# Cross-attention and a routed FFN on one core: x plus bias ahead of time, two chunk buffers, sums of P in turns

## The chip, the cores and the metric

One Trainium2 chip, one of its cores. The metric is the device time of the kernel in microseconds (us). The engines are TensorE (PE in rows; PEld are its weight loads), VectorE (DVE), ScalarE (ACT), GpSimd (POOL, here Pool) and SyncE (SP), which here only issues DMAs.

## What is computed

```python
x = x + xattn(ctx, layernorm(x))     # latents = layernorm(x): 2048 x 256; context 1601 x 192, masked
x = x + ffn(layernorm(x))            # 8 experts, the best 2 of each token

# xattn: 4 heads of 64
q = ln @ Wq.T;  k, v = split(concat([xn @ Wkv.T, ln @ Wlkv.T]))
attn = softmax(mask(rmsnorm(q, qn_g) * SCALE @ rmsnorm(k, kn_g).T))
out = (attn @ v) @ Wo.T + bo
# ffn
w, idx = top_k(softmax(x @ router.T), 2);  w = w / (w.sum() + 1e-6)
y = sum over the 2 experts of w * ((silu(x @ w1) * (x @ w3)) @ w2)
```

All arrays are float32.

## The kernel before

The kernel is written engine by engine, each with its own program in a fixed order; semaphores tie them together. NT = 16 tiles of 128 tokens, NC = 13 tiles of context, NK = 29 tiles of keys (context, then the latents themselves), NP = 15 pairs of key tiles.

*Prologue* (to about 160 us). For each of the 29 key tiles, in a pipeline of steps: normalise, transpose, project, write K^T (tiles S1, S2), V, and for latents Q^T (QT). x is loaded in one DMA into V[:, NC:NK], and ScalarE overwrites each of those tiles with its V (L532). Pool writes the mask column of each context tile (`k_mask`, L396 to 404) and waits for the transpose before the last in each step.

*Attention* (to about 840 us): UNITS = 16 units, u = 4 b + h: block b of 512 queries (QB = 4 tiles), head h. In each unit a loop over the 15 pairs p:

- TensorE: scores of pair p into one of two PSUM tiles bS (two products per key tile, L1238 and L1239), then, in odd steps, the products of P with V of pairs p-3 and p-2 (`outputs`, L1249). Between them stand 32 "pieces" of the score maxima of the *next* unit (`piece`, L1169), into two banks bM; VectorE reduces each (L862), and piece k waits for the reduction of piece k-2.
- ScalarE: P = exp(scores) into one of NPT = 4 buffers PT (L644). Before it may write buffer p % 4 it waits for the product with V of pair p-4 and for the sum that read it (`pt_free`, L597).
- The sum of P over keys, for the softmax: Pool adds pairs 0 to 10 into acc_p (ten instructions, L417, as `POOL_SUMS` says), VectorE adds pairs 11 to 14 into acc_d after its work on pieces (three instructions, L894), then merges the two (L900, L902).
- Weight splitting, six chunks of 128 x 256 per unit: SP loads a chunk of the expert weights into wraw[n % 2] (L323); ScalarE rounds it into whi (`w_hi`, L611, after the exponential of the pairs in `SPLIT_AT`), SP stores whi; Pool writes the rest, wraw - whi, into wraw (`w_lo`, L419, after the sums in `LO_AT`), SP stores that and then loads chunk n+2. `w_hi(n)` waits for chunk n's load, for the store of whi of chunk n-1 and for `w_lo(n-1)`.
- At p = 5 the output of the unit before is transposed and normalised (`o_T`, `o_out`); at p = 7 in even units two heads are transposed (`heads_T`, L1191) and ScalarE copies them into QT (L595), after its `w_hi` of that step.
- In units of blocks 1 to 3 (`w.fin`) one tile t of the block before is finished: x is loaded (`x_load`, p = 1, on ScalarE's queue), Pool adds the bias (L432), TensorE projects at p = 8 (L1196), VectorE adds and takes statistics (`stats2`, L907 to L911), ScalarE takes the square root (`sd`, p = 9, after its `w_hi`; the table of functions is loaded for it and again for the next exp), VectorE normalises at p = 10 (L917), TensorE transposes x3 at p = 11 (L1202), ScalarE copies it as x3T (L658, after its `w_hi`), TensorE multiplies by the router at p = 12 (L1208).

*Tail* (to about 912 us). The last QB = 4 tiles take the same steps together: SP loads x after the last product with V (L342 to L344), Pool adds the bias and makes the iotas (L439 to L450), and VectorE waits for the iotas first and then takes `stats2` and `norm` for each. ScalarE meanwhile issues the loads of the split weights of experts 0 to 3 (12.6 MB) ahead of its copy of the last output (L669 to L675). Then a long chain on VectorE routes the tokens (L972 to L1065), with the large table G at L1031.

*FFN* (to the end): 39 blocks of 128 rows: gather, three products per projection, scatter with add.

## Time and profile before

| | us |
|---|---|
| median of 3 runs | 1138.31 (1138.18 to 1139.41) |
| the profiled execution, its own time | 1141.2 |
| its span | 1139.2 |
| TensorE busy in the span | 983.2 (86%) |
| Pool, VectorE, ScalarE busy | 594.1, 653.5, 477.6 |

The rows further down are read like this. Times count from the span's start. An instruction in order of time has its start, its length, engine, line, operation and the tiles it writes and reads; `x8` means that eight were merged; in brackets stands how long the engine had been idle before it and who released it. "DMA x<-y" as a releaser is a transfer. A matmul's end is modelled, so the matmuls of a row overlap the next. 128x1024 is partitions by elements.

### The profile page before, as it was taken

Reading aid. Unit: us, or ns where it says so; the run is one execution under the profiler, and the core shown is the slowest. Engines: PE = TensorE matmul, PEld = TensorE weight load, DVE = VectorE, ACT = ScalarE, POOL = GpSimd, SP = SyncE. Lnnn points to the kernel's source line nnn. Section 1 sums busy time; section 2 is a strip of 40 time slices with the busy share of each in tenths; the row PEclk is TensorE's granted clock in tenths of the full one; section 3 lists DMA queues with packets and bytes.
Section 4 is the critical chain, followed back from the end, with each engine's and each line's share of the span. In section 5 each row is a group of like instructions: output and inputs, shape, how many; then the busy total and the mean of one; then the engine's idle time right before and its main releaser. Section 6 shows DMA issues by size and latency. Waiting matters only on the chain.

```text
span 1139.2 us, 15241 instructions
## 1 busy us (share of the span) xinstructions
PE 983.2 (86%) x4556; PEld 638.2 (56%) x4557; DVE 653.5 (57%) x1311; ACT 477.6 (42%) x751; POOL 594.1 (52%) x460
## 2 busy tenths in 40 slices
PE   2799779999999899898999999999882469999994
PEld 2565445555555555555554554555442458888883
DVE  3889776666666566566566566566125624444442
ACT  1456524455445446445455545454431022233231
POOL 4000018766974864854955855846820025556552
PEclk9899879999999999999999999999975579999998
DMA  6000002112111212121112212122169093332332
GB/s 173 1 1 1 9 5 72 54 56 70 61 61 65 71 55 70 57 69 65 61 61 70 65 56 75 56 65 75 56 262 367 16 360 48 54 51 51 51 52 27
DMA packets 66240, 85.15 MB, mean 75 GB/s; under 512 B 10283, under 2 KB 62444, under 8 KB 64140
## 3 DMA queue, kind: packets, MB, share of 16 engines
q1 hardware_dynamic: 49166, 56.57, 14.6%
q0 software_dynamic: 7488, 10.23, 5.5%
...
q8 instruction: 27, 0.44, 0.2%
q14 instruction: 25, 0.20, 0.1%
...
## 4 chain that ended last, share of the span: by engine, by line
PE 47%; POOL 20%; issue 10%; ACT 8%; DVE 8%; DMA 5%; ACTq 2%; DVEq 0%; POOLq 0%; SPq 0%
POOL acc_p L417 16%; PE bPV L1249 10%; ACT PT L644 5%; PE bS L1238 4%; PE bM L1169 4%; POOL wraw L421 4%; PE bS L1239 3%; PE bA L1116 3%; DMA x2t<-x 2%; PE bG L1328 2%; DVE mpart L862 2%; PE bH L1345 2%; PE bV L1133 2%; PE bG L1330 1%; PE bG L1329 1%
## 5 line engine op out<-in xcount | busy, mean ns | idle before, releaser
L862 DVE TENSOR_REDUCE mpart<-bM 128x1 f32<-128x464 f32 x492 | 295.6, 635 | 178.8 <-PE bM L1169 177.6
L417 POOL TENSOR_TENSOR acc_p<-acc_p,PT 128x1024 f32<-128x1024 f32 x144 | 343.8, 2387 | 33.6 <-ACT PT L644 29.3
L644 ACT ACTIVATE PT<-bS 128x1024 f32<-128x1024 f32 (+1 forms) x240 | 232.2, 993 | 64.8 <-PE bS L1239 58.4
L1249 PE MATMUL bPV<-PT,V 128*64 128x512 f32 x928 | 233.1, 610 | 0.0
L1238 PE MATMUL bS<-Q,S 128*128 128x512 f32 x464 | 190.0, 409 | 3.8 <-ACT PT L644 1.5
L1169 PE MATMUL bM<-S,Q 128*128 128x464 f32 x492 | 175.1, 414 | 12.1 <-DVE mpart L862 7.0
L1239 PE MATMUL bS<-Q,S 128*128 128x512 f32 x464 | 183.9, 396 | 0.0
L417 POOL TENSOR_TENSOR acc_p<-PT 128x1024 f32<-128x1024 f32 x16 | 41.6, 2601 | 255.9 <-ACT PT L644 255.9
L615 ACT CAST whi<-wraw 128x256 fp32r<-128x256 f32 x96 | 38.9, 405 | 248.3 <-POOL wraw L421 245.1
L1169 PEld LDWEIGHTS bM<-S,Q 128*128 128x128 f32 x492 | 85.0, 191 | 97.4 <-DVE mpart L862 67.6
L1238 PEld LDWEIGHTS bS<-Q,S 128*128 128x128 f32 x464 | 88.2, 190 | 56.6 <-issue 22.7
L1249 PEld LDWEIGHTS bPV<-PT,V 128*64 128x64 f32 x928 | 59.0, 136 | 104.9 <-issue 87.2
L1239 PEld LDWEIGHTS bS<-Q,S 128*128 128x128 f32 x464 | 88.1, 190 | 14.3
L478 POOL DMA_INDIRECT out<-ysb,ring_s x39 | 62.4, 1599 | 41.0 <-POOL ring_s L472 31.3
L421 POOL TENSOR_TENSOR wraw<-wraw,whi 128x256 fp32r<-128x256 f32 x96 | 70.5, 734 | 9.5 <-ACT whi L615 9.5
L1078 DVE TENSOR_TENSOR hs<-hs,bU 128x512 f32<-128x512 f32 x39 | 26.8, 688 | 63.6 <-PE bU L1330 62.1
L460 POOL COPY ring_g<-gidx 128x1 int32 (+1 forms) x39 | 27.6, 708 | 57.2 <-DVE sidx L1065 48.8
L463 POOL DMA_INDIRECT xg<-xln_d,ring_g x39 | 39.5, 1012 | 31.0 <-POOL ring_g L460 30.2
L696 ACT CAST hTe<-bH 128x512 fp32r<-128x512 f32 x39 | 22.9, 587 | 66.9 <-PE bH L1345 57.4
L708 ACT CAST xTe<-bXe 128x256 fp32r<-128x256 f32 x39 | 14.6, 374 | 85.7 <-PE bXe L1366 85.7
L1328 PE MATMUL bY<-W,hTe 128*128 x156 | 47.2, 303 | 1.5 <-DVE hTe L1072 1.5
L1329 PE MATMUL bY<-W,hTe 128*128 x156 | 44.0, 282 | 0.0
...
## 6 DMA issues: line engine op xcount, KB each, us to landing
wraw<-w SPq DMA_DIRECT2D x96, 128.0 KB, 2.3
wsp_d<-whi SPq DMA_DIRECT2D x96, 128.0 KB, 2.2
wsp_d<-wraw SPq DMA_DIRECT2D x96, 128.0 KB, 1.7
...
x<-x ACTq DMA_DIRECT2D x12, 128.0 KB, 2.0
out<-x ACTq DMA_DIRECT2D x12, 128.0 KB, 1.9
```

Of the source, the lines that this page charges most:

```text
L417: pool.tensor_tensor(acc_p[:], one, PT[:, q % NPT, :, :], ALU.add).then_inc(sem("z_p"), 1)
L421: pool.tensor_tensor(wraw[:, n % 2, :].bitcast(F32R), wraw[:, n % 2, :], whi[:].bitcast(F32), ALU.subtract).then_inc(sem("wsplit"), 1)
L463: pool.indirect_dma_start(xg[:, s.par, :], None, xln_d, bass.IndirectOffsetOnAxis(ap=ring_g[:, s.par:s.par + 1], axis=0))\
L478: pool.indirect_dma_start(out, bass.IndirectOffsetOnAxis(ap=ring_s[:, s.par:s.par + 1], axis=0), ysb[:, s.par, :], None, compute_op=ALU.add)\
L644: act.activation(PT[:, p % NPT, 0:n, :], bS[(w.h + p) % 2][:, 0:n, :], ACT.Exp).then_inc(sem("exp"), 1)
L862: dve.tensor_reduce(mpart[:, i, g:g + 1], banks[k % len(banks)][:, 0:PIECE], AX, ALU.max)\
L1169: pe.matmul(banks[k % len(banks)][:, 0:PIECE], Q2[:, h % 2, i * P:(i + 1) * P], S2[:, h, g * PIECE:(g + 1) * PIECE], start=True, stop=True ...
L1238: pe.matmul(bS[sl][:, b, :], S1[:, h, c * P:(c + 1) * P], Q1[:, h % 2, :], start=True, stop=False)
L1239: last = pe.matmul(bS[sl][:, b, :], S2[:, h, c * P:(c + 1) * P], Q2[:, h % 2, :], start=False, stop=True)
L1249: last = pe.matmul(bPV[b * D:(b + 1) * D, 0, :], V[:, c, h * D:(h + 1) * D], PT[:, p % NPT, b, :], start=c < 2, stop=c >= NK - 2, skip_gro ...
L1328: pe.matmul(out_ap, st_hi, w[:, e, 0, lo:lo + n], start=first, stop=False)
L1329: pe.matmul(out_ap, st_lo, w[:, e, 0, lo:lo + n], start=False, stop=False)
```

## The change

- *x plus bias*. In the prologue Pool adds bo to each of the 16 tiles of x, as they stand in V before V overwrites them, into a buffer xbs of two tiles, and SP stores them to a new DRAM tensor xb_d. ScalarE's copy of V for a latent tile waits for the add of that tile. All later loads of x read xb_d, and Pool's adds of the bias in the units and in the tail are gone. The mask loop on Pool is written out instead of looped.
- *Two chunk buffers*. whi has two halves; `w_hi(n)` waits for the store of whi of chunk n-2 and for `w_lo(n-2)`.
- *Early last x tiles*. x2t lies over the Q buffers of even heads, and ScalarE issues its four loads at p = 2 of the last unit. VectorE waits for the stores out of x2t before it writes G.
- *Sums*. Pool takes pairs (0, 1), 2, 3, 6, 7, 8, 10, 11, 12 (nine instructions), VectorE (4, 5), 9, 13, 14 (four), the first two of them at p = 7 and p = 11 of its loop, ahead of the reductions of that step. `w_lo` goes after Pool's sums number 1, 2, 3, 5, 6, 8 (counted from 0) instead of 1, 3, 5, 7, 9, 9.

```diff
@@ -108,6 +108,7 @@
           router_t, w13, w2, out):
+    xb_d = nc.dram_tensor("xb_d", [TOK, DIM], F32, kind="Internal").ap()
     xln_d = nc.dram_tensor("xln_d", [TOK, DIM], F32, kind="Internal").ap()
@@ -179,7 +180,6 @@
         rt = sb("rt", [P, 2, E], at=big)
-        bob = sb("bob", [P, DIM], at=big)
         lg = sb("lg", [P, NT, E], at=big)
@@ -189,6 +189,8 @@
         qn = sb("qn", [P, 2, DIM], at=t0)
+        bob = sb("bob", [P, DIM], at=t0)
+        xbs = sb("xbs", [P, 2, DIM], at=t0)
         m_u8 = sb("m_u8", [P, NC], U8, at=t0)
@@ -204,17 +206,19 @@
         t1 = ExitStack()
-        Q1 = sb("Q1", [P, 2, QW], F32R, at=t1)
-        Q2 = sb("Q2", [P, 2, QW], F32R, at=t1)
+        tq = ExitStack()
+        QQ = sb("QQ", [P, 2, 2, QW], F32R, at=tq)
+        Q1, Q2 = QQ[:, :, 0, :], QQ[:, :, 1, :]
+        tq.close()
+        x2t = sb("x2t", [P, 2 * QB, DIM], at=t1)
         PT = sb("PT", [P, NPT, 2, QW], at=t1)
...
         wraw = sb("wraw", [P, 2, WC], at=t1)
-        whi = sb("whi", [P, WC], F32R, at=t1)
+        whi = sb("whi", [P, 2, WC], F32R, at=t1)
         t1.close()
...
         t2 = ExitStack()
-        x2t = sb("x2t", [P, QB, DIM], at=t2)
         x3t = sb("x3t", [P, QB, DIM], at=t2)
@@ -308,6 +312,12 @@
+            xb = xb_d.rearrange("(t p) d -> t p d", p=P)
+            for t in range(NT):
+                sp.wait_ge(sem("xb"), t + 1)
+                sp.dma_start(xb[t, :, :], xbs[:, t % 2, :]).then_inc(sem(f"xb_st{t % 2}"), 16)
             sp.wait_ge(sem("klo"), NK)
@@ -327,7 +337,7 @@
                 sp.wait_ge(sem("whi"), n + 1)
-                sp.dma_start(wsp_d[e, 0, :, c:c + WC], whi[:].bitcast(F32)).then_inc(sem("wst_h"), 16)
+                sp.dma_start(wsp_d[e, 0, :, c:c + WC], whi[:, n % 2, :].bitcast(F32)).then_inc(sem(f"wst_h{n % 2}"), 16)
                 sp.wait_ge(sem("wsplit"), n + 1)
@@ -335,13 +345,9 @@
-            xt = x.rearrange("(t p) d -> t p d", p=P)
             ot = out[0:TOK, :].rearrange("(t p) d -> t p d", p=P)
...
             NF = NT - QB
-            sp.wait_ge(sem("pv"), NP * UNITS)
-            for i in range(QB):
-                sp.dma_start(x2t[:, i, :], xt[NF + i, :, :]).then_inc(sem(f"xin_t{i}"), 16)
             for i in range(QB):
@@ -397,11 +403,23 @@
                 pool.wait_ge(sem("mcol"), 1)
-                held()
                 pool.tensor_copy(knat[:, t.par, :, D + 1], mcol[:, bass.ds(t.v, 1)].to_broadcast([P, H]))\
...
-            run_steps(pool, 0, NC + 2, k_mask)
+            def x_bias(t):
+                if t >= 2:
+                    pool.wait_ge(sem(f"xb_st{t % 2}"), 16 * (t // 2))
+                pool.tensor_tensor(xbs[:, t % 2, :], V[:, NC + t, :], bob[:], ALU.add).then_inc(sem("xb"), 1)
+            pool.wait_ge(sem("c_bo"), 16)
+            for t in range(NC + 2):
+                k_mask(Step(None, t))
+                if t == 3:
+                    pool.wait_ge(sem("x_in"), 16)
+                if t >= 3:
+                    x_bias(t - 3)
+            for t in range(NC - 1, NT):
+                x_bias(t)
@@ -418,7 +436,7 @@
                 pool.wait_ge(sem("whi"), n + 1)
-                pool.tensor_tensor(wraw[:, n % 2, :].bitcast(F32R), wraw[:, n % 2, :], whi[:].bitcast(F32),
+                pool.tensor_tensor(wraw[:, n % 2, :].bitcast(F32R), wraw[:, n % 2, :], whi[:, n % 2, :].bitcast(F32),
                                    ALU.subtract).then_inc(sem("wsplit"), 1)
@@ -427,18 +445,11 @@
                             w_lo(SHARE * w.u + k)
-                    if n == XB_AT and w.fin:
-                        pool.wait_ge(sem("xin"), 16 * w.tile + 16)
-                        pool.tensor_tensor(x2[:], x2[:], bob[:], ALU.add).then_inc(sem("xb"), 1)
-            pool.wait_ge(sem("c_bo"), 16)
             run_units(unit)
...
             pool.wait_ge(sem("pv"), NP * UNITS)
-            NF = NT - QB
-            for i in range(QB):
-                pool.wait_ge(sem(f"xin_t{i}"), 16)
-                pool.tensor_tensor(x2t[:, i, :], x2t[:, i, :], bob[:], ALU.add).then_inc(sem("xb"), 1)
             pool.iota(iot_i[:], pattern=[[1, P]], base=0, channel_multiplier=0).then_inc(sem("iota"), 1)
@@ -529,6 +540,8 @@
                     act.wait_ge(sem("v_mm"), t.v + 1)
+                    if b == 'l':
+                        act.wait_ge(sem("xb"), t.back(NC).v + 1)
                     act.copy(V[:, bass.ds(t.v, 1), :].rearrange("p a d -> p (a d)"), bV[t.par][:, 0, 0:DIM])\
@@ -610,13 +623,19 @@
                 act.wait_ge(sem(f"raw{n % 2}"), 16 * (n // 2) + 16)
-                after(act, sem("wst_h"), 16 * n)
-                after(act, sem("wsplit"), n)
-                act.copy(whi[:], wraw[:, n % 2, :]).then_inc(sem("whi"), 1)
-            xt = x.rearrange("(t p) d -> t p d", p=P)
+                after(act, sem(f"wst_h{n % 2}"), 16 * (n // 2))
+                if n > 1:
+                    act.wait_ge(sem("wsplit"), n - 1)
+                act.copy(whi[:, n % 2, :], wraw[:, n % 2, :]).then_inc(sem("whi"), 1)
+            xt = xb_d.rearrange("(t p) d -> t p d", p=P)
             ot = out[0:TOK, :].rearrange("(t p) d -> t p d", p=P)
             xlt = xln_d.rearrange("(t p) d -> t p d", p=P)
+            def x_load_last():
+                act.wait_ge(sem("s_mm"), NP * (UNITS - 1))
+                for i in range(QB):
+                    act.dma_start(x2t[:, i, :], xt[NT - QB + i, :, :]).then_inc(sem(f"xin_t{i}"), 16)
@@ -646,6 +665,8 @@
                         x_load(w.tile)
+                    if p == 2 and w.last:
+                        x_load_last()
                     if p in SPLIT_AT:
@@ -660,14 +681,16 @@
+            for k in range(2):
+                act.wait_ge(sem(f"xb_st{k}"), 16 * NT // 2)
             q_hi(0, 0, 0)
...
-            act.wait_ge(sem("wst_h"), 16 * E * NCH)
             for k in range(2):
+                act.wait_ge(sem(f"wst_h{k}"), 16 * E * NCH // 2)
                 act.wait_ge(sem(f"wst{k}"), 16 * E * NCH // 2)
@@ -902,7 +925,6 @@
             def stats2(t, x_, y, st, mv):
-                dve.wait_ge(sem("xb"), t + 1)
                 dve.wait_ge(sem("y_mm"), t + 1)
@@ -922,7 +944,10 @@
                         o_out(u, (w.h - 1) % H, w.pairs)
+                    if p in DVE_AT:
+                        z_sum(w, DVE_AT.index(p))
                     if p == Y_AT and w.fin:
+                        dve.wait_ge(sem("xin"), 16 * t + 16)
                         stats2(t, x2[:], bT[:, 0, 0:DIM], st2[:], mv2[:])
@@ -939,7 +964,7 @@
                     maxima(v)
-                for n in range(ND):
+                for n in range(DVE_AT.index(NP), ND):
                     z_sum(w, n)
@@ -961,6 +986,7 @@
                 if i < QB:
+                    dve.wait_ge(sem(f"xin_t{i}"), 16)
                     stats2(NF + i, x2t[:, i, :], bFY[i][:, 0, 0:DIM], st2t[:, i, :], mv2t[:, i, :])
@@ -1028,6 +1054,7 @@
             R = 2 * NT
+            dve.wait_ge(sem("ox_t"), 16 * QB)
             link(dve.tensor_tensor(G[:], flat.unsqueeze(2).to_broadcast([P, R, NBLK + 1]),
@@ -1396,10 +1423,10 @@
 OUT_AT, HEADS_AT, Y_AT, SD_AT, X3_AT, X3T_AT, LG_AT = 5, 7, 8, 9, 10, 11, 12
-XB_AT = 2
-SPLIT_AT, LO_AT = (1, 3, 5, 7, 9, 11), (1, 3, 5, 7, 9, 9)
-POOL_SUMS = ((0, 1),) + tuple((-1, p) for p in range(2, 11))
-DVE_SUMS = ((11, 12), (-1, 13), (-1, 14))
+SPLIT_AT, LO_AT = (1, 3, 5, 7, 9, 11), (1, 2, 3, 5, 6, 8)
+POOL_SUMS = ((0, 1),) + tuple((-1, p) for p in (2, 3, 6, 7, 8, 10, 11, 12))
+DVE_SUMS = ((4, 5), (-1, 9), (-1, 13), (-1, 14))
+DVE_AT = (7, 11, NP, NP)
 assert sum(sum(x) for x in PIECES) == NM and len(PIECES) == NP
```

## Rows read from the trace of the kernel before

**Rows 1.** Busy time by stretch: stretch, length, busy us (instructions) per engine, TensorE clock, DMA.
```profile
237.70:276.40 38.70, 38.59 (x175) 22.35 (x174) 25.51 (x42) 19.13 (x27) 28.25 (x16) 1.00 0.20 63
...
489.70:533.50 43.80, 40.93 (x185) 23.71 (x186) 26.96 (x48) 22.60 (x31) 28.76 (x17) 1.00 0.19 63
```

**Rows 2.** TensorE in order of time, an even unit: start, length, instruction [idle before, releaser].
```profile
507.06 0.39 PE L1238 MATMUL bS<-Q,S 128*128 128x512 f32 x1
...
514.99 1.10 PE L1196 MATMUL bT<-wot,QT 128*128 128x256 f32 x4 [1.44 <-ACT QT L595]
...
516.14 0.40 PE L1238 MATMUL bS<-Q,S 128*128 128x512 f32 x1
...
517.88 0.48 PE L1169 MATMUL bM<-S,Q 128*128 128x464 f32 x1 [0.44 <-DVE mpart L862]
...
527.84 0.61 PE L1208 MATMUL bT<-rt,x3T 128*128 128x8 f32 x4 [0.86 <-ACT x3T L658]
```

**Rows 3.** TensorE in order of time, an odd unit.
```profile
478.46 0.44 PE L1202 MATMUL bT<-ident,x 128*128 128x128 f32 x2 [1.32 <-DVE x L917]
...
484.05 0.61 PE L1208 MATMUL bT<-rt,x3T 128*128 128x8 f32 x4 [1.15 <-ACT x3T L658]
```

**Rows 4.** ScalarE in order of time, the even unit of rows 2.
```profile
513.96 0.40 ACT L615 CAST whi<-wraw 128x256 fp32r<-128x256 f32 x1 [3.27 <-POOL wraw L421]
...
517.27 1.02 ACT L644 ACTIVATE PT<-bS 128x1024 f32<-128x1024 f32 x1 [1.50 <-PE bS L1239]
...
527.11 0.40 ACT L615 CAST whi<-wraw 128x256 fp32r<-128x256 f32 x1 [2.41 <-POOL wraw L421]
```

**Rows 5.** SP's DMA issues in that unit; then the page's row: count, KB, us to landing.
```profile
502.32 0.32 SPq L332 DMA_DIRECT2D wsp_d<-wraw  x1
504.39 0.33 SPq L323 DMA_DIRECT2D wraw<-w  x1
```

```profile
wraw<-w SPq DMA_DIRECT2D x96, 128.0 KB, 2.3
```

**Rows 6.** Groups by line: shapes, count, busy us, mean ns, idle before and releasers.
```profile
L417 POOL TENSOR_TENSOR acc_p<-acc_p,PT 128x1024 f32<-128x1024 f32 x144 | 343.8, 2387 | 33.6 <-ACT PT L644 29.3
...
L894 DVE TENSOR_TENSOR acc_d<-PT 128x1024 f32<-128x1024 f32 x16 | 19.4, 1216 | 0.6 <-ACT PT L644 0.6
...
L856 DVE TENSOR_TENSOR Q<-QT,Q 64x512 fp32r<-64x512 f32 x16 | 12.9, 809 | 1.2 <-ACT Q L578 0.9
...
L401 POOL COPY knat<-mcol 128x4 f32 (+1 forms) x15 | 2.8, 190 | 60.3 <-PE bK L1144 54.3 <-DVE mcol L808 6.0
```

**Rows 7.** Pool, VectorE and TensorE in order of time, around `q_lo` in unit 0.
```profile
165.49 2.45 POOL L417 TENSOR_TENSOR acc_p<-PT 128x1024 f32<-128x1024 f32 x1 [88.14 <-ACT PT L644]
...
165.75 2.74 DVE L856 TENSOR_TENSOR Q<-QT,Q 64x512 fp32r<-64x512 f32 x1
...
169.09 0.47 PE L1169 MATMUL bM<-S,Q 128*128 128x464 f32 x1 [2.13 <-DVE mpart L862]
```

**Rows 8.** VectorE and Pool in order of time, the even unit of rows 2.
```profile
508.40 0.64 DVE L862 TENSOR_REDUCE mpart<-bM 128x1 f32<-128x464 f32 x1 [0.16 <-PE bM L1169]
...
508.30 4.86 POOL L417 TENSOR_TENSOR acc_p<-acc_p,PT 128x1024 f32<-128x1024 f32 x2
```

**Rows 9.** The tail in order of time, of several engines.
```profile
832.72 0.73 POOL L421 TENSOR_TENSOR wraw<-wraw,whi 128x256 fp32r<-128x256 f32 x1 [0.59 <-ACT whi L615]
...
837.34 4.17 ACTq L674 DMA_DIRECT2D W<-wsp_d  x8
...
847.81 6.36 PE L1196 MATMUL bFY<-wot,QT 128*128 128x256 f32 x16 [0.77 <-ACT QT L595]
...
861.17 0.72 POOL L441 TENSOR_TENSOR x2t<-x2t,bob 128x256 f32<-128x256 f32 x1 [3.32 <-DMA x2t<-x]
...
867.59 0.41 DVE L907 TENSOR_TENSOR x2t<-x2t,bFY 128x256 f32<-128x256 f32 x1
...
872.70 0.19 DVE L969 COPY lg<-bL 128x32 f32<-128x32 f32 x1 [2.94 <-PE bL L1208]
```

## The prediction

> **What bounds the kernel now.** I read the table of the span by stretch first, then TensorE's own instructions in order of time in one unit of each kind, then the order of ScalarE and Pool in the same unit, then the tail. In a unit of the first block TensorE is busy 38.59 of 38.70 us; in a unit of a later block it is busy 40.93 of 43.80 us [rows 1]. Both hold the full clock (1.00). So the first four units are limited by TensorE's own work, and the other twelve have holes on top of a little more work. The holes of an even unit are three waits of TensorE: 1.44 us before the projection (for QT, copied by ScalarE), 0.44 us before a piece of the maxima (for VectorE), 0.86 us before the routing product (for x3T, copied by ScalarE) [rows 2]. In an odd unit they are 1.32 us for x3 and 1.15 us for x3T [rows 3].
>
> Why is ScalarE late? Just before each of those copies it stands in `w_hi`, waiting for Pool: 3.27 us before the cast at 513.96, 2.41 us before the one at 527.11 [rows 4]. There is one `whi` buffer, so the cast of chunk n waits for Pool's subtraction of chunk n-1, and Pool does that only after a sum of P that takes 2.39 us [rows 6]. The copy for the projection stands behind the cast at 513.96 in ScalarE's program, x3T behind the one at 527.11, and in odd units the square root for x3 behind the same kind of wait. The chain is therefore Pool, then ScalarE's order, then TensorE.
>
> In the tail the last four tiles of x are only asked for when the last unit is over. Pool waits for them, adds the bias until 861.2 + 0.7, and VectorE starts afterwards, while TensorE's projection ran from 847.81 for 6.36 us [rows 9]. So here the loads of x set the time.
>
> **Part 1: two chunk buffers.** `w_hi(n)` waits for chunk n-2 instead of n-1. What is next late is the raw chunk: after Pool's subtraction SP stores it, and issues the next load into that buffer 2.07 us after the store's issue; the load takes 2.3 us more [rows 5]. A raw chunk is thus ready 4.4 us after the subtraction of the chunk two before. I walked the even unit, in its own times. The first subtraction ends at 502.3 as now (its store is issued then) [rows 5]; then the sum of pair 3 and its subtraction, until 505.4 (2.39 + 0.73). The raw chunks for `w_hi` at p = 5 and 7 are there at 506.7 and 509.8. Exponentials 6 and 7 run at about 508.2 to 510.3, so the cast at p = 7 doesn't wait and the copy of QT is done at about 511.4. TensorE reaches the projection 1.44 us before 514.99, at 513.5: that wait goes. Downstream the cast at p = 9 waits about 1 us for its raw chunk (ready at 517.8), the square root ends at 519.9, x3 at 520.8, and TensorE wants x3 at about 521.1. The cast at p = 11 has its chunk in time and x3T is there about 1 us before it is wanted. So both waits of an even unit and both of an odd one go, with only 0.3 us to spare at x3; the 0.44 us stays, since VectorE's own statistics of x2 cause it.
>
> The gain is 1.44 + 0.86 = 2.30 us in each of the six even units 4 to 14, and 1.32 + 1.15 = 2.47 us in each of the five odd ones 5 to 13: 13.8 + 12.4 = 26.2 us. Idle time is counted from the modelled end of the matmul before, so up to 0.15 us more per wait (22 x 0.15 = 3.3 us) may come. In units 0 to 3 nothing is won: TensorE has no hole.
>
> **Part 2: nine sums on Pool, four on VectorE.** Pool loses one sum of 2.39 us [rows 6] and (part 3) the bias add of 0.72 us per unit (as in the tail) [rows 9]; it is not the limit of a unit by its total, so nothing is gained directly. VectorE gets one more sum, 1.22 us [rows 6]; it is busy about 27 of 43.8 us [rows 1]. The new sums stand at p = 7 and 11, before the four pieces of that step, and TensorE waits for pieces. After the piece of p = 6 VectorE is free at 508.40 + 0.64 = 509.04 [rows 8]; sum (4, 5) runs to 510.3, the two pieces issued at 509.5 and 509.7 are reduced by 511.6, and TensorE's next piece comes only after its product with V, at 511.9. The cover is that product. So the sum costs nothing if it starts at once.
>
> Does it? Here is the speaking row against the change. In unit 0 VectorE's subtraction `q_lo` took 2.74 us [rows 7], where the other fifteen took (16 x 0.809 - 2.74) / 15 = 0.68 us [rows 6]. It began at 165.75, inside Pool's sum of 165.49 to 167.94, and ended 0.55 us after that sum; TensorE then waited 2.13 us for the pieces behind it [rows 7]. Both have two operands in SBUF. A reduction of VectorE, which reads PSUM, is not held: the one at 508.40 took 0.64 us inside Pool's sums from 508.30 on [rows 8]. So a sum of P on VectorE that arrives inside one on Pool would wait for its rest. The Trainium skill states this as a rule ("SBUF — State Buffer", section "Who interferes with whom"): a VectorE instruction with two SBUF inputs and a GpSimd instruction that reads SBUF exclude each other, and whoever starts first keeps the ports for the whole instruction. By that rule, the trace agrees.
>
> Who is first is set by one matmul group, scores 6 at 507.06. Exponentials start 1.13 us after the issue of their scores (516.14 to 517.27) [rows 2, 4] and take 1.03 us, so Pool's sum of pair 6 cannot start before 509.2, while VectorE starts at about 509.05; Pool's last work before was done at 505.4. VectorE is first by 0.15 to 0.3 us, and Pool then waits about 1.1 us, which it can: it has nearly 4 us of slack before its next sums. At p = 11 the table loads hold exponential 10 back to about 521.3, and VectorE is first by 0.8 us in later blocks, by 0.3 us in units 0 to 3. At the unit's end the sum of pair 13 meets Pool's last sum and waits up to 1.6 us, but the maxima stand before it and the next unit wants VectorE only 1.5 us after its start. Cost taken: 0.
>
> **Part 3: x plus bias in the prologue.** Sixteen adds of 0.72 us [rows 9] (11.5 us) go to Pool, which sat idle 54.3 us in the same loop waiting for transposes [rows 6], and sixteen stores to SP, whose program has nothing there between the first loads and the first chunk. ScalarE's V copy waits for the add of its tile; adds run at one per context step, a dozen steps ahead of the latent tiles. The adds may meet VectorE's normalisation (a tensor-scalar, SBUF to SBUF); the trace has no case of the two together. I take 1 us, bounds 0 and 11.5 (all sixteen, one behind the other). The Trainium skill says, same page and section, that tensor_scalar can enter a mode that takes the shared ports; by it each of the eleven or so adds in the context steps could cost up to its 0.72 us, 7.9 us in all.
>
> **Part 4: early last tiles.** Four loads are issued by ScalarE at p = 2 of the last unit, into the idle Q buffers. With x there, VectorE follows the projection: last tile at 847.81 + 6.36 = 854.2. From the last add to the logits is 872.70 - 867.59 = 5.1 us [rows 9], so the logits come at 859.3 instead of 872.7: 13.4 us less. The iotas move ahead too. The new wait for the stores of x2 stands before G, which comes 15 us after the logits, at about 874; behind it on VectorE is all of the routing. Those stores share the DMA engines with the loads of W and are issued from 850 on; the four x tiles landed about 4 us apart under that load (Pool's adds, the last at 861.17 [rows 9]). At that pace eight stores would end near 873 to 882, less once the W loads are over. I take 0, bound 4 us.
>
> The last unit has no pieces, so it is led by Pool and by ScalarE's casts. Its end is fixed by the last subtraction (832.72 + 0.73), its store, ScalarE's 4.17 us of issuing W, and then the copy of the output [rows 9]. Pool has one sum and one add less; later positions of the subtractions eat most of that. I take 1 us, bounds -4 and +2.
>
> **Sum.** 26.2 + 13.4 + 1 - 1 = 39.6 us off the profiled 1141.2 us (span 1139.2) gives 1101.6; the runs' median, 1138.3, is 2.9 us lower, so 1098.7, call it 1099. Its own range, from the bounds above, is 1089 to 1107.
>
> **Rivals.** (a) *The load of the raw chunk takes the place of the wait.* The 0.3 us at x3 is thin. If casts at p = 9 and 11 wait 1.2 us longer than I have it, eleven units lose that: 1099 + 13 = 1112. For: the 4.4 us round trip is real. Against: only one cast per unit meets it in my walk.
>
> (b) *The waits at TensorE stay altogether* and only the tail gains: 1099 + 26 = 1125. Against: rows 4 put ScalarE's wait right before each late copy. This is also the case in which the change doesn't do what it says.
>
> (c) *Pool is first at p = 7.* VectorE waits up to 2.39 us and reduces the pieces at 513.4 and 514.0 instead of by 511.6; TensorE loses about 2.1 us, the price that unit 0 paid (2.13) [rows 7]. Fifteen units: 31 us, 1130.
>
> (d) *Pool is first at both places*, the one that ends slower: 30 x 2.1 = 63 us, 1162. It decides once the loss per unit passes 2.7 us, that is, once both sums lose the race in most units. For: the margin is only tenths. Against: VectorE and Pool are released by the same scores, in an order that repeats.
>
> **Chances.** Forecast 0.55, (a) 0.15, (b) 0.08, (c) 0.09, (d) 0.08, and 0.05 for below 1089. The range 1088 to 1130 takes the forecast, (a), (b) and half of (c), 0.8. All but (d) and the top of (c) are faster: faster 0.90, same 0.02, slower 0.08, with 0.2% (2.3 us) as the least that can be told from no change here.
>
> **What would show it.** Right: units of later blocks 41.1 to 41.5 us apart instead of 43.7; no idle time before the projection, x3 and routing products, 0.44 us still before the piece; ScalarE's casts waiting for Pool a small part of today's total; VectorE's sums still 1.2 us long at p = 7 and 11, and Pool's third-from-first sum (pair 6) and its sum of pair 10 about 1 us longer; no DMA wait in the tail, logits about 5 us after the projection. Wrong: casts idle on DMA (a); VectorE's sums of 3 us and more with TensorE idle on pieces behind them (c, d); a wait of several us before G; a prologue that ends more than 1 us later than 165 us.

## The result and the profile after

The changed kernel takes 1091.68 us (median, 1091.33 to 1092.64) beside 1138.86 us for the kernel before on the same chip: a ratio of 0.9586, 95% interval 0.957 to 0.9603, 47.2 us less. Its profiled execution took 1091.53 us with a span of 1089.6, against 1141.2 and 1139.2. The forecast was 1099 us, between 1088 and 1130.

First the table of the span by stretch (stretch, length, busy us (instructions) of PE, PEld, DVE, ACT and POOL, TensorE's clock, DMA share, GB/s): a unit of the first block, an even and an odd unit of a later one. It answers to [rows 1].

```profile
236.26:274.99 38.73, 38.62 (x174) 22.38 (x173) 28.32 (x43) 19.67 (x27) 27.02 (x15) 1.00 0.20 62
476.26:517.24 40.98, 40.42 (x183) 23.84 (x182) 29.55 (x49) 22.90 (x31) 27.71 (x16) 1.00 0.21 68
517.24:557.76 40.52, 39.94 (x179) 23.46 (x179) 29.43 (x49) 22.36 (x30) 27.57 (x16) 1.00 0.22 69
```

The first block is as it was. In the even unit the idle part of TensorE fell from 43.80 - 40.93 = 2.87 us to 0.56; in the odd unit, against the odd one of before that ends at 489.70 (43.72 us long, 40.67 busy), from 3.05 to 0.58. Two gaps with a named releaser are left in these two later units, one in each, TensorE in order of time; those of [rows 2] and [rows 3] at the projection, x3 and x3T are gone:

```profile
502.82 0.47 PE L1196 MATMUL bM<-S,QQ 128*128 128x464 f32 x1 [0.45 <-DVE mpart L885]
543.36 0.47 PE L1196 MATMUL bM<-S,QQ 128*128 128x464 f32 x1 [0.45 <-DVE mpart L885]
```

ScalarE's casts say where the waits went, the page's group for them (count, busy us, mean ns, idle before and releaser), in the kernel before and then in the changed one. The idle time ahead of them was nearly all behind Pool's subtraction; what is left is behind the raw chunk's load:

```profile
L615 ACT CAST whi<-wraw 128x256 fp32r<-128x256 f32 x96 | 38.9, 405 | 248.3 <-POOL wraw L421 245.1
```

```profile
L629 ACT CAST whi<-wraw 128x256 fp32r<-128x256 f32 x96 | 38.6, 402 | 75.1 <-DMA wraw<-w 74.6
```

VectorE and Pool in order of time, in that even unit, around the two sums that moved:

```profile
495.57 1.22 DVE L917 TENSOR_TENSOR acc_d<-PT 128x1024 f32<-128x1024 f32 x1
...
507.78 1.21 DVE L917 TENSOR_TENSOR acc_d<-acc_d,PT 128x1024 f32<-128x1024 f32 x1
...
515.29 3.69 DVE L917 TENSOR_TENSOR acc_d<-acc_d,PT 128x1024 f32<-128x1024 f32 x2
```

```profile
495.97 3.05 POOL L435 TENSOR_TENSOR acc_p<-acc_p,PT 128x1024 f32<-128x1024 f32 x1 [4.04 <-ACT PT L663]
...
508.58 2.66 POOL L435 TENSOR_TENSOR acc_p<-acc_p,PT 128x1024 f32<-128x1024 f32 x1 [3.39 <-ACT PT L663]
...
516.72 1.71 POOL L439 TENSOR_TENSOR wraw<-wraw,whi 128x256 fp32r<-128x256 f32 x1
```

VectorE is first at both places and its sums keep 1.2 us, here and in all of the units 0 to 14; Pool's sum that starts inside takes 3.05 and 2.66 us instead of 2.39 [rows 6]. At the unit's end each side waits about a microsecond for the other (3.69 us for two sums, 1.71 for a subtraction of 0.73).

The tail in order of time, ScalarE's issue of W, its copy of the output, VectorE's first and last add of the four tiles, and the logits, to be held against [rows 9]:

```profile
801.69 4.33 ACTq L697 DMA_DIRECT2D W<-wsp_d  x8
806.11 0.58 ACT L602 COPY oT_a<-bPV 128x512 f32<-128x512 f32 x1 [9.38 <-issue]
```

```profile
815.13 0.42 DVE L929 TENSOR_TENSOR x2t<-x2t,bFY 128x256 f32<-128x256 f32 x1 [3.17 <-PE bFY L1223]
...
819.81 0.41 DVE L929 TENSOR_TENSOR x2t<-x2t,bFY 128x256 f32<-128x256 f32 x1
...
823.69 0.19 DVE L995 COPY lg<-bL 128x32 f32<-128x32 f32 x1 [1.71 <-PE bL L1235]
```

The ledger of the span, in us. A unit is taken to end where its last row of products with V starts, 199.32 in unit 0 before. "Copy" is ScalarE's copy of the last output; it began at 841.61 before.

| stretch | before | after | gain | forecast |
|---|---|---|---|---|
| prologue and unit 0, to 199.32 / 197.95 | 199.32 | 197.95 | 1.4 | -1 |
| units 1 to 3 | 115.37 | 115.34 | 0 | 0 |
| units 4 to 14, from 314.69 / 313.29 | 481.16 | 448.45 | 32.7 | 26.2 |
| last unit, up to the copy | 45.76 | 44.37 | 1.4 | 1 |
| copy to logits | 31.09 | 17.58 | 13.5 | 13.4 |
| logits to the end | 266.5 | 265.9 | 0.6 | 0 |
| sum | 1139.2 | 1089.6 | 49.6 | 39.6 |

The 1.4 us of unit 0 aren't the change's. In the kernel before, TensorE stood idle for 2.13 us behind `q_lo` [rows 7], and its granted clock then fell to 0.50 (the level of 1.2 GHz) for 3.4 us; in the changed kernel the wait was 1.46 us and the clock stayed at 1.00. First the stretch from 171 to 173 us before, then after:

```profile
171.00:173.00 2.00, 2.00 (x6) 0.83 (x3) 0.09 (x1) 0.41 (x1) 2.00 (x2) 0.50 0.19 66
```

```profile
171.00:173.00 2.00, 2.00 (x10) 1.24 (x7) 0.91 (x2) 0.00 (x0) 2.00 (x2) 1.00 0.19 66
```

But the first experiment below, which up to there is the changed kernel, waited 2.19 us, fell to 0.50 as well and ended unit 0 within 0.2 us of the kernel before. The length of the wait follows how far `q_lo` starts inside Pool's first sum: 0.26 us behind its start before (2.74 us long), 0.50 in the changed kernel (2.50), 0.18 in that experiment (2.81). In three of the experiments' profiles the clock fell there, in the others it didn't; what sets the start wasn't found.

### The profile page after: what moved, and what is told of

Its sections match the earlier page's. It is cut to its first block, busy times and chain, and to the rows that moved or that the text cites. A ratio compares the mean times of both kernels' runs of the same rounds, so it can differ in the third digit from the quotient of the medians.

```text
span 1089.6 us, 15244 instructions
## 1 busy us (share of the span) xinstructions
PE 971.0 (89%) x4556; PEld 637.0 (58%) x4557; DVE 697.3 (64%) x1327; ACT 483.6 (44%) x751; POOL 589.3 (54%) x444
## 4 chain that ended last, share of the span: by engine, by line
PE 71%; DVE 6%; issue 4%; ACT 2%; DMA 2%; POOL 1%; ACTq 1%; POOLq 0%; DVEq 0%
PE bPV L1276 20%; PE bM L1196 10%; PE bS L1265 9%; PE bS L1266 8%; DVE mpart L885 2%; PE bG L1355 2%; PE bH L1372 2%; PE bY L1355 2%; PE bY L1356 2%; PE bY L1357 2%; PE bG L1357 2%; PE bG L1356 2%; PE bU L1357 2%; PE bU L1355 2%; PE bT L1211 2%
## 5 line engine op out<-in xcount | busy, mean ns | idle before, releaser
L435 POOL TENSOR_TENSOR acc_p<-acc_p,PT 128x1024 f32<-128x1024 f32 x128 | 321.8, 2514 | 108.4 <-ACT PT L663 104.6
L663 ACT ACTIVATE PT<-bS 128x1024 f32<-128x1024 f32 (+1 forms) x240 | 237.0, 996 | 191.0 <-PE bS L1266 184.9
L1276 PE MATMUL bPV<-PT,V 128*64 128x512 f32 x928 | 230.6, 604 | 0.0
L1265 PE MATMUL bS<-QQ,S 128*128 128x512 f32 x464 | 189.9, 409 | 2.4 <-ACT QQ L595 0.7
L1196 PE MATMUL bM<-S,QQ 128*128 128x464 f32 x492 | 174.8, 414 | 11.6 <-DVE mpart L885 6.4
L1266 PE MATMUL bS<-QQ,S 128*128 128x512 f32 x464 | 183.8, 396 | 0.0
L1196 PEld LDWEIGHTS bM<-S,QQ 128*128 128x128 f32 x492 | 84.9, 192 | 95.4 <-DVE mpart L885 70.3
L1265 PEld LDWEIGHTS bS<-QQ,S 128*128 128x128 f32 x464 | 87.9, 189 | 53.9 <-issue 26.0
L1266 PEld LDWEIGHTS bS<-QQ,S 128*128 128x128 f32 x464 | 87.9, 190 | 14.4
L439 POOL TENSOR_TENSOR wraw<-wraw,whi 128x256 fp32r<-128x256 f32 x96 | 86.4, 900 | 0.0
L917 DVE TENSOR_TENSOR acc_d<-acc_d,PT 128x1024 f32<-128x1024 f32 (+1 forms) x48 | 79.7, 1660 | 2.8 <-ACT PT L663 2.3
L629 ACT CAST whi<-wraw 128x256 fp32r<-128x256 f32 x96 | 38.6, 402 | 75.1 <-DMA wraw<-w 74.6
L1355 PE MATMUL bY<-W,hTe 128*128 x156 | 47.2, 303 | 1.5 <-DVE hTe L1099 1.5
## 6 DMA issues: line engine op xcount, KB each, us to landing
W<-wsp_d SPq DMA_DIRECT2D x8, 1536.0 KB, 12.6
```

The source lines that it names most:

```text
L435: pool.tensor_tensor(acc_p[:], one, PT[:, q % NPT, :, :], ALU.add).then_inc(sem("z_p"), 1)
L439: pool.tensor_tensor(wraw[:, n % 2, :].bitcast(F32R), wraw[:, n % 2, :], whi[:, n % 2, :].bitcast(F32), ALU.subtract).then_inc(sem("wsplit ...
L663: act.activation(PT[:, p % NPT, 0:n, :], bS[(w.h + p) % 2][:, 0:n, :], ACT.Exp).then_inc(sem("exp"), 1)
L917: dve.tensor_tensor(acc_d[:, 0:m, :], one, PT[:, q % NPT, 0:m, :], ALU.add).then_inc(sem("z_d"), 1)
L1196: pe.matmul(banks[k % len(banks)][:, 0:PIECE], Q2[:, h % 2, i * P:(i + 1) * P], S2[:, h, g * PIECE:(g + 1) * PIECE], start=True, stop=True ...
L1265: pe.matmul(bS[sl][:, b, :], S1[:, h, c * P:(c + 1) * P], Q1[:, h % 2, :], start=True, stop=False)
```

## The experiments

Each is an edit of the changed kernel. Times are medians, ratios are to the kernel before, with a 95% interval. "A pair of units" is one even and one odd unit of blocks 1 to 3; it takes 87.5 us before and 81.5 after.

**Late loads of the last x tiles.**

```diff
@@ SP, after its last chunk
+            for k in range(2):
+                sp.wait_ge(sem(f"xb_st{k}"), 16 * NT // 2)
+            sp.wait_ge(sem("pv"), NP * UNITS)
+            for i in range(QB):
+                sp.dma_start(x2t[:, i, :], xb[NF + i, :, :]).then_inc(sem(f"xin_t{i}"), 16)
@@ ScalarE, unit
-                    if p == 2 and w.last:
-                        x_load_last()
```

> The changed kernel with only the last four x tiles loaded late: SP issues the loads after the last product with V, as in the kernel before (x plus bias still comes from the prologue, so Pool adds nothing). My theory: the last landing, some 20 us after the issue, sets the end of the tail again, and the logits come 12 to 14 us later: about 1105 us. Rival: most of what the tail won came from Pool's adds and iotas that stood behind the loads, and late loads alone cost under 6 us: below 1098.

Measured: 1091.48 us (1090.31 to 1092.91), ratio 0.9578 [0.9562, 0.9594]: the early loads are worth nothing in this kernel, and the 12 to 14 us of the theory were wrong. SP and ScalarE, in order of time, show why:

```profile
801.68 1.80 SPq L355 DMA_DIRECT2D x2t<-xb_d  x4
```

```profile
803.04 4.43 ACTq L695 DMA_DIRECT2D W<-wsp_d  x8
```

Before, x was asked for 2.6 us after the issue of W began (839.97 against 837.34 [rows 9]); here 1.4 us before it. The last products with V now end well before the last subtraction's store, for which W waits, so that even a load behind the products is ahead of W.

**One chunk buffer, sums in turns.**

```diff
@@ w_hi
-                after(act, sem(f"wst_h{n % 2}"), 16 * (n // 2))
-                if n > 1:
-                    act.wait_ge(sem("wsplit"), n - 1)
-                act.copy(whi[:, n % 2, :], wraw[:, n % 2, :]).then_inc(sem("whi"), 1)
+                after(act, sem("wst_h"), 16 * n)
+                after(act, sem("wsplit"), n)
+                act.copy(whi[:, 0, :], wraw[:, n % 2, :]).then_inc(sem("whi"), 1)
... the same buffer and semaphore at SP's store, Pool's subtraction and ahead of W's loads
```

> The changed kernel with one whi buffer (the cast of chunk n waits for the store and the subtraction of chunk n-1), its sums in turns kept. My theory: the waits of TensorE before projection, x3 and router come back, and since the new places of the subtractions come later (after the sums of pairs 6, 8, 10) each cast waits longer than in the kernel before: 3 to 4 us per unit of the later blocks, so 1122 to 1136 us. Rival, that the turns alone free ScalarE's order: under 1105 us.

Measured: 1119.35 us (1118.1 to 1121.18), ratio 0.9832 [0.9815, 0.9848], below the expected range by 2.6 us. The second buffer is worth 27.7 us in the changed kernel. The casts' group is back at

```profile
L628 ACT CAST whi<-wraw 128x256 fp32r<-128x256 f32 x96 | 38.8, 405 | 210.7 <-POOL wraw L439 175.0 <-DMA wsp_d<-whi 35.5
```

and with it the waits at the projection (0.68 us, for QT), at x3 (0.74 us) and for x3T (0.88 us in an even unit, 1.16 in an odd one). The casts wait for 210.7 us in all, less than before (248.3) and not more, which the theory had the other way.

**The old dealing of the sums, two chunk buffers.**

```diff
-SPLIT_AT, LO_AT = (1, 3, 5, 7, 9, 11), (1, 2, 3, 5, 6, 8)
-POOL_SUMS = ((0, 1),) + tuple((-1, p) for p in (2, 3, 6, 7, 8, 10, 11, 12))
-DVE_SUMS = ((4, 5), (-1, 9), (-1, 13), (-1, 14))
-DVE_AT = (7, 11, NP, NP)
+SPLIT_AT, LO_AT = (1, 3, 5, 7, 9, 11), (1, 3, 5, 7, 9, 9)
+POOL_SUMS = ((0, 1),) + tuple((-1, p) for p in range(2, 11))
+DVE_SUMS = ((11, 12), (-1, 13), (-1, 14))
+DVE_AT = (NP, NP, NP)
```

> The changed kernel with the old split of the sums (Pool pairs 0 to 10, VectorE 11 to 14 at the end of the unit, subtractions at their old places), two chunk buffers kept. My theory: with two buffers the dealing of the sums in turns is worth next to nothing, since Pool's ten sums and six subtractions (28 us) fit into a unit of 41 us and each buffer PT is read before it is wanted: 1089 to 1096 us. Rival: Pool is nearly saturated from pair 0 to pair 10 and holds the exponentials up: 10 us or more slower, over 1101 us.

Measured: 1100.97 us (1099.57 to 1101.3), ratio 0.9661 [0.9645, 0.9677]: 9.3 us slower than the changed kernel. The theory missed; dealing in turns does gain. A pair of units takes 82.8 us; the last unit's products end later (39.7 us instead of 34.3), but from its start to the copy of the output it takes 44.5 us against 44.4, so the loss lies in the units before it. The casts wait longer for raw chunks, 97.4 us against 74.6, and most of the difference is at p = 7, 1.6 us a unit instead of 0.1:

```profile
L629 ACT CAST whi<-wraw 128x256 fp32r<-128x256 f32 x96 | 38.7, 403 | 98.1 <-DMA wraw<-w 97.4
```

and the wait at x3, whose 0.3 us of room the forecast called thin, is there again, in TensorE's order of time:

```profile
553.01 0.44 PE L1229 MATMUL bT<-ident,x 128*128 128x128 f32 x2 [0.45 <-DVE x L939]
```

This is rival (a) in small: in the changed kernel the second subtraction stands behind the sum of pair 3 and not behind that of pair 4, so that the raw chunk for p = 7 is loaded sooner. Whether the dealing of the sums matters beyond these places isn't told apart; this run puts both back.

**One chunk buffer and the old dealing.** Both diffs above.

> The changed kernel with one whi buffer and the old split of the sums: what is left is x plus bias in the prologue and the early x tiles. My theory: the waits of TensorE in the twelve later units are back at 2.8 and 3.2 us per unit (33 us), less a little, because Pool's bias add no longer delays its first subtractions: 1117 to 1125 us. Rival: the bias add on Pool was what made the casts late; then the units stay near 41 us and the time is under 1105 us.

Measured: 1119.54 us (1118.6 to 1121.63), ratio 0.9831 [0.9815, 0.9848], as expected. With one buffer the dealing is worth nothing (1119.35 and 1119.54); the 9.3 us are there only with two. A pair of units takes 86.3 us, 1.2 us less than before though neither part 1 nor part 2 is in: the one piece of work in the units that still differs is the bias add, which Pool no longer does. (That this is the cause is argued from what is left; no run puts the add alone back with one buffer.)

**The same, with late loads of x.** The first diff on top.

> From the changed kernel: one whi buffer, the old dealing of the sums, and the loads of the last four x tiles back on SP behind the last pair's PV; only the prologue's x plus bias is left of the change. Theory (the early loads are worth their 13 us only while the last unit is the long one of 41 us: then ScalarE's sixteen loads of W go out about 2.6 us before SP's four of x, as before, and the x tiles land behind them): o_copy to logits is 30 to 31 us again, the whole about 13 us above e4_both_old, 1131 to 1135 us, near 6 us under the kernel before. Rival (the tail shrank because the x tiles no longer pass Pool's bias add and were read from another place, not because they were loaded early): within 3 us of e4_both_old, 1117 to 1122 us. A profile with SP's x loads ahead of ScalarE's W loads would speak for neither.

Measured: 1127.5 us (1125.88 to 1128.68), ratio 0.9895 [0.988, 0.991], 8.0 us over the run before it: between the two expectations, so each was half of it. VectorE's adds in the tail, in order of time, follow the landings one by one:

```profile
843.38 0.42 DVE L926 TENSOR_TENSOR x2t<-x2t,bFY 128x256 f32<-128x256 f32 x1 [3.16 <-PE bFY L1220]
...
846.74 0.42 DVE L926 TENSOR_TENSOR x2t<-x2t,bFY 128x256 f32<-128x256 f32 x1 [2.27 <-DMA x2t<-xb_d]
...
855.41 0.42 DVE L926 TENSOR_TENSOR x2t<-x2t,bFY 128x256 f32<-128x256 f32 x1 [3.02 <-DMA x2t<-xb_d]
```

The last tile is there 21.3 us after SP's first issue (834.10), as before (839.97 to 861.17 [rows 9]). But from the copy to the logits it takes 24.5 us (836.00 to 860.53), where it took 31.1 before and takes 17.5 with early loads. In the kernel before, VectorE did nothing for any tile until this, in order of time:

```profile
862.29 0.33 DVE L957 CAST iot<-iot_i 128x128 f32<-128x128 int32 x1 [16.41 <-POOL pc_i L444]
```

Pool's iotas stood behind its four bias adds, and VectorE waits for the iotas first, so three landed tiles lay idle. So taking the adds off Pool, and with it the iotas' early place, gave 6.6 us of the tail (31.1 to 24.5), the early loads 7.0 (24.5 to 17.5), and these only while W is asked for first. Whether the iotas ahead of the adds would have done for the first part wasn't run.

**An extra instruction on VectorE, two SBUF operands.** In units 0 to 14, ahead of the step of pair 8.

```diff
+                    if p == 8 and not w.last:
+                        dve.wait_ge(sem("z_d"), ND * u + 1)
+                        dve.tensor_tensor(acc_d[:], acc_d[:], acc_d[:], ALU.max).then_inc(sem("extra"), 1)
+                    if p == 10 and not w.last:
+                        dve.wait_ge(sem("extra"), u + 1)
```

> The changed kernel with one more VectorE instruction per unit (but the last) at p = 8, while Pool is inside a sum of P: acc_d = max(acc_d, acc_d), 128x1024, two operands in SBUF, the result unchanged. My theory (such an instruction waits for the rest of Pool's instruction): it takes 2.5 to 3.6 us instead of 1.2, and TensorE waits on pieces for 2 to 3 us more per unit, 25 to 45 us in all. Rival (the 2.74 us of q_lo in unit 0 had another cause): it takes 1.2 us and the unit loses 0.3 to 1.2 us, under 18 us in all.

Measured: 1144.66 us (1142.18 to 1145.67), ratio 1.0036 [1.0024, 1.0047], 53 us over the changed kernel: the direction as expected, the size larger than the 25 to 45 us; why is said below.

**The same place, one SBUF operand.** The added line is now `dve.tensor_reduce(junk[:], acc_d[:], AX, ALU.max)`.

> The same place and the same tile as e5_extra_two_sbuf, but a reduction of acc_d into a small tile of its own: one operand in SBUF, 128x1024 read. My theory: it runs beside Pool's sum, takes about 1.2 us, and the unit loses only what its own length costs, 0.3 to 1.2 us, 5 to 18 us in all. Rival (any VectorE read of SBUF waits for Pool): as long and as dear as in e5_extra_two_sbuf.

Measured: 1097.65 us (1096.99 to 1098.32), ratio 0.9634 [0.9595, 0.9672], 6.0 us over, as expected. The groups of the two added lines, first the one with two operands, then the one with one:

```profile
L951 DVE TENSOR_TENSOR acc_d<-acc_d 128x1024 f32<-128x1024 f32 x15 | 46.0, 3065 | 0.0
```

```profile
L952 DVE TENSOR_REDUCE junk<-acc_d 128x2 f32<-128x1024 f32 x15 | 18.1, 1209 | 0.0
```

Same place, same 1024 columns: 3065 ns against 1209. One case of the first, VectorE in order of time, and then Pool's tile's own answer for the two sums there (shortest, median and longest in ns, first and last start):

```profile
480.66 3.41 DVE L951 TENSOR_TENSOR acc_d<-acc_d 128x1024 f32<-128x1024 f32 x1
```

```profile
L435 POOL TENSOR_TENSOR acc_p<-acc_p,PT x2: 2374/2794/3214, 480.6 to 483.1; 128x1024 f32<-128x1024 f32 x2
```

VectorE began 0.05 us after Pool's first sum. That sum kept its 2.37 us, and VectorE, which had to wait for it, ended 1.1 us behind it. Pool's next sum started at 483.1, inside VectorE's instruction, and took 3.21 us, 0.8 more than usual: it is now the one that waits. So it is in fourteen of the fifteen units; in unit 0 VectorE was first and took 1.22 us.

The price of arriving second isn't one number. Over the run with one operand, units 2 and 3 became 1.8 and 2.2 us longer (41.25 and 41.27 against 39.46 and 39.05), with the clock at 1.00 in all four; TensorE waited 2.25 and 2.69 us for the piece in them. Unit 1 and the units from 4 on lost 3.3 to 3.9 us, and in these TensorE's granted clock fell. In the case above TensorE waited 2.80 us for the piece behind VectorE's instruction, and then ran at 0.50, the level of 1.2 GHz, for 3.4 us; TensorE in order of time, and a stretch of it:

```profile
485.65 0.47 PE L1201 MATMUL bM<-S,QQ 128*128 128x464 f32 x1 [2.80 <-DVE mpart L885]
```

```profile
487.00:489.00 2.00, 2.00 (x8) 0.44 (x4) 0.00 (x0) 0.89 (x1) 0.00 (x0) 0.50 0.19 66
```

What decides between the two kinds isn't shown; their mean is (53 - 6) / 15 = 3.1 us a unit.

**Statistics behind the reduction.**

```diff
-                    if p == Y_AT and w.fin:
-                        dve.wait_ge(sem("xin"), 16 * t + 16)
-                        stats2(t, x2[:], bT[:, 0, 0:DIM], st2[:], mv2[:])
                     if not w.last:
                         for _ in range(sum(PIECES[p])):
                             piece(v, k, M_BANKS)
                             k += 1
+                    if p == Y_AT and w.fin:
+                        dve.wait_ge(sem("xin"), 16 * t + 16)
+                        stats2(t, x2[:], bT[:, 0, 0:DIM], st2[:], mv2[:])
```

> From the changed kernel: in the twelve units with a tile of x to finish, VectorE's residual sum and statistics of that tile stand behind its reduction of the projection piece of pair 8 and not ahead of it. Theory (each 0.1 us by which VectorE's order holds TensorE in a unit is on the path now): TensorE's 0.61 us before the piece behind the projection goes in twelve units, 5 to 8 us in all, 1084 to 1087 us. Rival (ScalarE's casts and exps or Pool's sums set the unit by now, and TensorE's gap only moves to the next wait): less than 2 us, 1090 to 1093 us.

Measured: 1085.99 us (1084.77 to 1087.32), ratio 0.9536 [0.9523, 0.9549], as expected: 5.7 us for the last named gap of TensorE. A pair of units takes 80.3 us on the mean, 1.2 less, for two brackets of 0.45 us.

**The copy of the output ahead of W's loads.**

```diff
+            o_copy(UNITS)
             for k in range(2):
                 act.wait_ge(sem(f"wst_h{k}"), 16 * E * NCH // 2)
                 act.wait_ge(sem(f"wst{k}"), 16 * E * NCH // 2)
             ...
-            o_copy(UNITS)
```

> From the changed kernel: behind the last pair ScalarE copies the last outputs first and then waits for the stores of the split W and issues its loads. Theory (ScalarE's copy of the last outputs stands idle behind Pool's last low half and its store, from 797 to 804.9): the copy comes 4 to 7 us earlier, the projections and the four tiles' statistics with it, and the end comes 3 to 6 us earlier, 1086 to 1089 us. Rival (the routing waits for something else, the x tiles or the loads of W, which now start at the same time as before): under 1 us, 1090.5 to 1092 us.

Measured: 1090.66 us (1089.8 to 1091.39), ratio 0.9577 [0.9564, 0.959]. The logits come at 818.36 instead of 823.69, 5.3 us earlier, as the theory has it, and the end doesn't follow. The wait of G, from its tile's own answer:

```profile
  DMA out<-x2t: 4.0, 1
```

Its stores of x2 are issued behind W, from SP: the median from issue to landing is 17.1 us. The rival holds, with its place: it is the wait which the forecast of part 4 bounded at 4 us. In the changed kernel the last of these stores lands at 837.68 and G starts at 838.62, so the tail had 0.9 us to give and no more.

**Three moves.** The two diffs above, and `q_lo` ahead of the reductions of p = 1.

> From the changed kernel: the moves of e8_stats_after_piece and e9_copy_before_w, and VectorE's low half of Q ahead of the first pieces' reductions of each unit instead of behind them. Theory: the parts add, 5 to 8 and 3 to 6 us, and the low half no longer meets Pool's first sum in unit 0 (1.5 to 2 us less there, 0 elsewhere): 1076 to 1082 us. Rival (the moved low half holds the first reductions, and TensorE waits for a free bank in every unit): 0.3 to 0.5 us a unit back, 1083 to 1090 us.

Measured: 1090.75 us (1088.15 to 1091.36), ratio 0.9576 [0.9563, 0.9589]. In unit 0 `q_lo` takes 0.69 us instead of 2.50 and unit 0 ends 2.2 us sooner (195.75 against 197.95), but every later unit pays, as the rival has it. TensorE in order of time has one such wait of 0.5 to 0.6 us in each, here in a later unit:

```profile
481.86 0.47 PE L1196 MATMUL bM<-S,QQ 128*128 128x464 f32 x1 [0.63 <-DVE mpart L885]
```

and units 1 to 3 take 38.81, 39.23 and 38.80 us instead of 38.31, 38.73 and 38.30. G waits 4.3 us here.

**The bias add back on Pool.**

```diff
+                    if n == 2 and w.fin:
+                        pool.wait_ge(sem("xin"), 16 * w.tile + 16)
+                        pool.tensor_tensor(x2[:], x2[:], x2[:], ALU.add).then_inc(sem("xm"), 1)
@@ VectorE
-                        dve.wait_ge(sem("xin"), 16 * t + 16)
+                        dve.wait_ge(sem("xm"), t + 1)
```

> From the changed kernel: part 3 undone for Pool alone. In each of the twelve units with a tile of x, Pool adds x to itself behind its sum of pair 3, where the kernel before added the bias, and VectorE's sum of the residual waits for it; the residual of those tiles is so 2x, the rest as before. Theory (Pool has no time to spare between pair 3 and pair 8 any more, 0.7 us more there delays each low half and each later sum): up to 0.7 us a unit, at most 8, of which ScalarE's casts with two buffers hide most; 1092 to 1096 us. Rival (Pool's order isn't on the path with two buffers): within 0.7 us of 1091.7. Below 1091 us would speak against both.

In those tiles the kernel adds x (with its bias) twice, so that its output is another; it stands here for its time alone. Measured: 1091.88 us (1091.01 to 1093.4), ratio 0.9585 [0.9568, 0.9602]: the rival. With two buffers and the sums in turns the add costs nothing; with one buffer and the old dealing its absence gave, as argued above, 1.2 us a pair.

**Statistics behind the reduction, and W's loads last.** The diff of the statistics; W's six lines move from ahead of `o_copy(UNITS)` to behind the exp of the routing:

```diff
             act.activation(ra[:], rb[:], ACT.Exp).then_inc(sem("r_ex"), 1)
+            for k in range(2):
+                act.wait_ge(sem(f"wst_h{k}"), 16 * E * NCH // 2)
+                act.wait_ge(sem(f"wst{k}"), 16 * E * NCH // 2)
+            for e in range(EARLY):
+                ...
```

> From the changed kernel: the move of e8_stats_after_piece, and ScalarE issues its eight loads of W (12.6 MB, which take 29 us to land and are read from 871 on) behind the exp of the routing and not ahead of the copy of the last outputs. Theory (the copy ahead gives 5.3 us up to the logits, which e9_copy_before_w lost again in a wait of 4.0 us for the stores of the last rows, queued behind the loads of W; now these stores are ahead of them): 5 to 6 us below e8_stats_after_piece, 1079 to 1082 us, no wait before G. Rival (the wait before G stays, or the loads of W now land late for the first expert): 1084 to 1088 us, with the wait seen at G or at the first matmuls that read W.

Measured: 1081.32 us (1079.12 to 1081.93), ratio 0.9487 [0.9469, 0.9505], inside the expected 1079 to 1082 and 4.7 us below the run with the statistics alone (5 to 6 expected), and the fastest version here. The issues by tile (count, KB, median us to landing) show the stores of the last rows ahead of W; G doesn't wait, and the first product that reads W waits for the gathered rows and not for W:

```profile
W<-wsp_d ACTq DMA_DIRECT2D x8, 1536.0 KB, 25.5
...
out<-x2t SPq DMA_DIRECT2D x4, 128.0 KB, 2.3
```

```profile
861.79 0.79 PE L1356 MATMUL bG<-W,xTe 128*128 x1 [1.12 <-DVE xTe L1109]
```

## Where the prediction was right and wrong

**What bounds the kernel.** Right. The chain from Pool by ScalarE's order to TensorE was the one: with one buffer back, ScalarE stands 175 us behind Pool again and 27.7 us are lost.

**Part 1.** The mechanism was right at each step: the waits at the projection, x3 and x3T went, the 0.45 us for the piece stayed, units 1 to 3 didn't move. The walk held to half a microsecond. The casts of an even unit, ScalarE in order of time, start at p = 5, 7 and 9 at

```profile
493.24 0.41 ACT L629 CAST whi<-wraw 128x256 fp32r<-128x256 f32 x1 [3.03 <-DMA wraw<-w]
496.86 0.40 ACT L629 CAST whi<-wraw 128x256 fp32r<-128x256 f32 x1
504.09 0.41 ACT L629 CAST whi<-wraw 128x256 fp32r<-128x256 f32 x1 [0.88 <-DMA wraw<-w]
```

which, with the unit's start moved from 476.26 to 489.70, is 506.7, 510.3 and 517.5, where the walk had the chunks ready at 506.7, 509.8 and 517.8. Only the remark that one cast per unit meets the load was wrong: two do, and the longer wait, at p = 5, costs TensorE nothing.

The term was too small: 32.7 us measured in units 4 to 14 against 26.2. TensorE's idle time fell by 2.31 us in the even unit and by 2.47 in the odd one, which are the 2.30 and 2.47 of the sum; but the units became 2.82 and 3.20 us shorter. The other 0.51 and 0.73 us are time that the table counts as busy, 6 x 0.51 + 5 x 0.73 = 6.7 us in all, which is the 6.5 that the term lacked. The forecast named this and gave it 3.3 us at most. The starts of successive products show it: against the changed kernel, the even unit of before falls behind by 1.68 us at the projection, bracket 1.44, and by 1.13 at the routing product, bracket 0.86. So a wait costs more than its bracket, and the bracket should have been checked against starts of instructions.

Nor is the 32.7 us the second buffer's alone, as the heading of the part has it. By the profiles, units 4 to 14 take 481.2 us before, 475.8 without the bias add (one buffer, old dealing), 456.4 with the second buffer and 448.5 with the new dealing: 5, 19 and 8 us in this order. In the other order the dealing gives 2 and the buffer 25. In medians the second buffer takes 18.6 us off on the old dealing (1119.54 to 1100.97) and 27.7 on the new.

**Part 2.** "It is not the limit of a unit by its total, so nothing is gained directly" was the step that failed. With two buffers the dealing is worth 9.3 us. A total says nothing on when Pool's subtractions come, and these set the raw chunk's next load. Without it, x3 waits 0.45 us, which the walk had put at 0.3 us of room. The walk for part 1 used the new place of the second subtraction (behind the sum of pair 3), so its 26.2 us already held this gain; the text then gave the gain to the buffer and nothing to the dealing. The race was forecast right: VectorE first at both places, by 0.4 us at p = 7; Pool's sum of pair 6 is 0.66 us longer as forecast in kind, that of pair 10 only 0.27. Rivals (c) and (d) were real dangers. Their 2.1 us for a late arrival is what one at p = 8 cost while the clock stayed at 1.00 (1.8 and 2.2 us). What they left out is the clock: where it fell, in twelve of the fourteen units, the price was 3.3 to 3.9. Two late arrivals in each unit weren't run; by these prices, an estimate, (d) would have cost more than its 63 us.

**Part 3.** Cost taken 1 us, measured none: the first reduction of maxima starts at 140.8 in the new kernel and at 140.9 in the old. The upper end, 11.5 us, didn't come, nor did 7.9 us; but the two do meet. Only one of the sixteen normalisations of x started well inside one of Pool's adds, and it took 0.73 us where the rest took 0.40; VectorE and then Pool (two adds of 0.72 and 0.73, the second from 77.57 to 78.30) in order of time:

```profile
77.71 0.73 DVE L774 TENSOR_SCALAR xn<-V,mvs,rsd 128x256 f32<-128x256 f32 x1
```

```profile
76.89 1.41 POOL L412 TENSOR_TENSOR xbs<-V,bob 128x256 f32<-128x256 f32 x2
```

A small one at 79.79 took 0.35 us instead of 0.17, and those of VectorE that read PSUM were not longer beside the adds (0.41 us). The Trainium skill says that tensor_scalar can take the shared ports ("SBUF — State Buffer", section "Who interferes with whom"); on these two cases the trace agrees. It cost about 0.5 us in all, because the others didn't start inside an add, and nothing at the end of the prologue. What the forecast left out is that the add's absence gains: 1.2 us a pair with one buffer, and 6.6 us in the tail.

**Part 4.** 13.4 us forecast, 13.5 measured; that they agree to a tenth is luck in part, and for half of it the cause was wrong. "So here the loads of x set the time" holds for the last tile alone; the first three had landed and lay behind the iotas, which stood behind Pool's adds. The text saw that the iotas move ahead, and gave them nothing. And in the changed kernel the early loads do nothing, since the shorter last unit lets a late load pass ahead of W as well. Two errors cancel in the sum: the last add came 13.7 us behind the copy and not 12.6, and from it to the logits it took 3.9 us and not 5.1; TensorE's granted clock was 1.00 in that stretch, and 0.50 in the same one before. The wait before G was 0 as taken, with 0.9 us to spare; its bound of 4 us was about right once the tail got shorter (4.0 and 4.3). The last unit's term, 1 us, came out at 1.4: TensorE ends 7.0 us sooner there, and ScalarE still waits for the last subtraction's store before W.

**The sum.** 39.6 us forecast, 49.6 in the profiles: 6.5 from part 1's term with part 2's share in it, 2.4 from unit 0 and the prologue, 1.1 from the rest. Of the 2.4 us, 1.0 is the cost of part 3 that didn't come, and the 1.4 isn't owed to the change, as said under the ledger: the gap behind `q_lo` and whether the clock fell after it differ between runs with the same code up to there. In medians the forecast is 7.3 us too high; the difference to 10 is that the profiled execution before was 2.9 us slower than its median and the one after was not. The end was inside the range. The forecast's "own range" of 1089 to 1107 doesn't follow from its bounds: added up, these give about 1093 to 1118, and the result lies just below, by the part of the brackets that was bounded too low and by unit 0.
